# First layer's experts: both products of the 128-slot blocks from plain float32 operands

## What is computed

```python
logits = xf @ gate_w                        # 8 experts, each token takes its best 2
comb   = softmax weights of the best 2, scattered to (tokens, 8)
h   = gelu(einsum('nd,edf->enf', xf, W1) + b1[:, None, :], approximate=False)   # 256 -> 1024
y   = einsum('enf,efd->end', h, W2) + b2[:, None, :]                             # 1024 -> 256
out = einsum('ne,end->nd', comb, y)
```

## Time and profile before

| | |
|---|---|
| median of 3 runs | 838.35 us (836.78 to 839.5) |
| span of the profiled execution, first to last instruction | 836.6 us |
| first layer's experts, loads to last output issue | 225 to 497 us of the span |
| PE busy | 750.5 us (90%) |
| DVE busy | 609.3 us (73%) |
| ACT busy | 477.6 us (57%) |
| POOL busy | 386.1 us (46%) |

### The profile page before, as it was taken

How to read it: one execution, slowest core, us unless ns; L and a number is a source line. 1 busy time by engine, 2 the same in 40 slices (tenths; PEclk the granted TensorE clock), 3 DMA queues, 4 the chain that set the end, 5 groups by cost and what they waited for, 6 DMA issues and landing times. The chain is left out here.

```text
span 836.6 us, 17408 instructions
## 1 busy us (share of the span) xinstructions
PE 750.5 (90%) x6872; PEld 633.6 (76%) x6872; DVE 609.3 (73%) x1212; ACT 477.6 (57%) x722; POOL 386.1 (46%) x379
## 2 busy tenths in 40 slices
PE   6999999999469999999999948999999998359995
PEld 5666676667359999999999947667676667359995
DVE  4777776753769998998998925777776752869982
ACT  3386666654057776776776613586666753536640
POOL 5465444122145766666666335565542112183532
PEclk9999999999769999999999988999999999669998
DMA  7001000010286888888788327000000000477732
GB/s 227 16 27 40 27 17 13 28 52 27 71 308 199 260 253 259 257 255 258 250 244 261 89 33 228 14 15 27 15 15 14 15 15 26 154 263 244 214 86 28
DMA packets 45521, 101.35 MB, mean 121 GB/s; under 512 B 9824, under 2 KB 36064, under 8 KB 37760
## 3 DMA queue, kind: packets, MB, share of 16 engines
q0 software_dynamic: 16800, 65.46, 26.7%
q1 hardware_dynamic: 28640, 34.78, 12.7%
HBM read 84.22 MB, written 15.74 MB: 119 GB/s over the span
## 5 line engine op out<-in xcount | busy, mean ns | idle before, releaser
L600 DVE TENSOR_REDUCE mx_a<-ps_max_a 128x2 f32<-128x512 f32 x256 | 164.1, 684 | 35.4 <-PE ps_max_a L846 35.1
L89 PE MATMUL ps_h_e<-xe_t_e,w_e 128*128 128x256 f32 (+1 forms) x480 | 137.8, 287 | 9.8 <-DVE xe_t_e L1770 9.8
L452 ACT ACTIVATE prob_a<-ps_st_a 128x2048 f32<-128x2048 f32 x64 | 120.1, 1877 | 29.0 <-PE ps_st_a L865 28.6
L90 PE MATMUL ps_h_e<-xe_t_e,w_e 128*128 128x256 f32 (+1 forms) x480 | 134.6, 281 | 0.0
L91 PE MATMUL ps_h_e<-xe_t_e,w_e 128*128 128x256 f32 (+1 forms) x480 | 134.6, 280 | 0.0
L89 PE MATMUL ps_y_e<-w_e,h_e 128*128 128x256 f32 x424 | 118.2, 279 | 0.0
L91 PE MATMUL ps_y_e<-w_e,h_e 128*128 128x256 f32 x424 | 117.7, 278 | 0.0
L90 PE MATMUL ps_y_e<-w_e,h_e 128*128 128x256 f32 x424 | 117.7, 278 | 0.0
L89 PEld LDWEIGHTS ps_h_e<-xe_t_e,w_e 128*128 128x128 f32 x480 | 92.7, 193 | 12.3 <-DVE xe_t_e L1770 12.2
L91 PEld LDWEIGHTS ps_h_e<-xe_t_e,w_e 128*128 128x128 f32 x480 | 92.4, 193 | 0.0
L90 PEld LDWEIGHTS ps_h_e<-xe_t_e,w_e 128*128 128x128 f32 x480 | 92.3, 192 | 0.0
(11 more groups left out here) (234 smaller groups left out, 1763.1 us busy)
## 6 DMA issues: line engine op xcount, KB each, us to landing
w_raw_w<-L_w SPq DMA_DIRECT2D x14, 1024.0 KB, 6.6
ctx_raw_a<-ctx_t SPq DMA_DIRECT2D x16, 256.0 KB, 4.7
normalised_weighted<-xr SPq DMA_DIRECT2D x16, 256.0 KB, 2.2
x_sb<-x SPq DMA_DIRECT2D x8, 256.0 KB, 4.8
x_sb<-x SPq DMA_DIRECT2D x2, 1024.0 KB, 8.5
x<-x_sb SPq DMA_DIRECT2D x8, 256.0 KB, 2.5
out<-x_sb SPq DMA_DIRECT2D x4, 512.0 KB, 7.7
q_s_a<-m_t_a SPq DMA_DIRECT2D x64, 4.0 KB
```

Source lines behind the costliest of these rows:

```text
L89: pe.matmul(out, lhs[0], rhs[0], start=start, stop=False)
L90: pe.matmul(out, lhs[1], rhs[0], start=False, stop=False)
L452: act.activation(prob[n % 2][:, :, :, :], ps_st[:, :, :, :], ACT.Exp, scale=HD ** -0.5).then_inc(prob_ready, 1)
L600: dve.tensor_reduce(mx[:, q, h:h + HG + 1:HG], ps_max[j][:, :, :], AX.X, ALU.max).then_inc(max_done, 1)
```

## The change

In the first layer the seven small blocks take both products straight from unsplit float32 operands. The first product reads `w1_raw` and a plain copy of the transposed tokens (`xe_plain`), one matmul where `split_matmul` made three; the second reads a plain `h_plain`, which the gelu writes directly, and `w2_raw`. Nothing is rounded or subtracted for a small block: `w1_high`, `w1_low`, `w2_high`, `w2_low`, `hidden_parts` and the subtraction of `inputs_low` return at once; only the two bias copies stay on DVE. Since PE now reads the raw buffers, they are free later: `w1_raw` of a small block when its first product is done, `w2_raw` when its second is. POOL's order follows: `load_w1` of F2, which wants S's buffer, goes to the end of S's turn, and `load_w2` of F2 to the end of F1's turn. The full blocks and the second layer compute as before.

```diff
     xe_t = [[sb(f"xe_t{i}{j}", [P, KC, SB], F32R) for j in range(2)] for i in range(2)]
+    if layer == 0:
+        xe_plain = sb("xe_plain", [P, KC, P])
+    more = sb("more", [P, MORE])
+    h_plain = more[:, 0:FC * P].rearrange("p (j s) -> p j s", j=FC)
...
@@ -1569,11 +1580,15 @@
         def load_w1(b):
             if b < blocks:
                 pool.wait_ge(w1_ready, b - 1)
+                if small(b - 2):
+                    pool.wait_ge(h_ps, (b - 1) * NP)
                 gather_weights(pool, "w1", buffers, shared, dram, b)
 
         def load_w2(b):
             if b < blocks:
                 wait(pool, w2_ready, b - 1)
+                if b >= 2 and small(b - 2):
+                    pool.wait_ge(y_ps, b - 1)
                 gather_weights(pool, "w2", buffers, shared, dram, b)
...
         else:
             for b in range(blocks):
-                load_w1(b + 2)
-                load_w2(b + 1)
+                if not small(b):
+                    load_w1(b + 2)
+                if b == 0 or not small(b - 1):
+                    load_w2(b + 1)
                 load_x(b + 2)
                 if b >= 2:
                     add_to_tokens(b - 2)
+                if small(b):
+                    load_w1(b + 2)
+                if b and small(b - 1):
+                    load_w2(b + 1)
...
         def hidden(b, jp):
             act.wait_ge(h_ps, b * NP + jp + 1)
-            wait(act, h_ready, b * NP + jp - 1)
+            if small(b):
+                if jp == 0:
+                    wait(act, y_ps, max([c + 1 for c in range(b) if small(c)], default=0))
+                for j in range(2):
+                    ins = act.activation(h_plain[:, 2 * jp + j, :], ps_h[jp % RB][:, j, 0:P], ACT.Gelu,
+                                         bias=b1[b % 2][:, 2 * jp + j:2 * jp + j + 1])
+                ins.then_inc(hid_ready, 1)
+                return
...
         def inputs_high(b):
             act.wait_ge(xe_ps, b + 1)
-            w = order[b][2] * P
-            act.activation(xe_t[b % 2][0][:, :, 0:w], ps_x[b % 2][:, :, 0:w], ACT.Copy).then_inc(xe_hi, 1)
+            if small(b):
+                wait(act, h_ps, max([(c + 1) * NP for c in range(b) if small(c)], default=0))
+                act.activation(xe_plain[:, :, :], ps_x[b % 2][:, :, 0:P], ACT.Copy).then_inc(xe_hi, 1)
+            else:
+                act.activation(xe_t[b % 2][0][:, :, :], ps_x[b % 2][:, :, :], ACT.Copy).then_inc(xe_hi, 1)
...
     def dve_part(dve):
+        def small_bias(b):
+
+            dve.wait_ge(w1_ld[b % 2], loaded(b))
+            wait(dve, hid_ready, (b - 1) * NP)
+            dve.tensor_copy(b1[b % 2][:, :], w1_raw[b % 2][:, KC * F:KC * F + FC]).then_inc(w1_ready, 1)
+
         def w1_low(b, k):
-            dve.wait_ge(w1_hi, b * KC + k + 1)
+            if small(b):
+                if k == KC - 1:
+                    small_bias(b)
+                return
+            dve.wait_ge(w1_hi, splits(b) * KC + k + 1)
...
         def w2_low(b, k):
-            dve.wait_ge(w2_hi, b * 2 + k + 1)
+            if small(b):
+                if k == 1:
+                    dve.wait_ge(w2_ld[b % 2], loaded(b))
+                    wait(dve, y_biased, b - 1)
+                    dve.tensor_copy(b2[b % 2][:, :], w2_raw[b % 2][:, FC * D:FC * D + D]).then_inc(w2_ready, 1)
+                return
+            dve.wait_ge(w2_hi, splits(b) * 2 + k + 1)
...
         def hidden_parts(b, jp):
+            if small(b):
+                return
...
-                dve.tensor_reduce(slot_weight[:, b, 0:n], by_expert[:, 0:n, :], AX.X, ALU.add)
-            dve.tensor_tensor(xe_t[b % 2][1][:, :, 0:n * P], ps_x[b % 2][:, :, 0:n * P], xe_t[b % 2][0][:, :, 0:n * P].bitcast(F32),
-                              ALU.subtract).then_inc(xe_ready, 1)
+                ins = dve.tensor_reduce(slot_weight[:, b, 0:n], by_expert[:, 0:n, :], AX.X, ALU.add)
+            if not small(b):
+                ins = dve.tensor_tensor(xe_t[b % 2][1][:, :, :], ps_x[b % 2][:, :, :], xe_t[b % 2][0][:, :, :].bitcast(F32),
+                                        ALU.subtract)
+            ins.then_inc(xe_ready, 1)
...
                     for k in range(KC):
+                        if small(b):
+                            ins = pe.matmul(ps_h[jp % RB][:, j, 0:w],
+                                            w1_raw[b % 2][:, k * F + (2 * jp + j) * P:k * F + (2 * jp + j + 1) * P],
+                                            xe_plain[:, k, :], start=k == 0, stop=k == KC - 1)
+                            continue
                         ins = split_matmul(pe, ps_h[jp % RB][:, j, 0:w], [w1[b % 2][s][:, k, 2 * jp + j, :] for s in range(2)],
                                            [xe_t[b % 2][s][:, k, 0:w] for s in range(2)], k == 0, k == KC - 1)
...
         def second_product(b):
             pe.wait_ge(w2_ready, b + 1)
-            pe.wait_ge(h_ready, (b + 1) * NP)
+            if small(b):
+                pe.wait_ge(hid_ready, (b + 1) * NP)
+            else:
+                pe.wait_ge(h_ready, (splits(b) + 1) * NP)
             wait(pe, y_ready if layer else y_biased, b - 1)
...
                 for j in range(FC):
+                    if small(b):
+                        ins = pe.matmul(bank[:, q, :], h_plain[:, j, :], w2_raw[b % 2][:, j * D:(j + 1) * D], start=j == 0, stop=j == FC - 1)
+                        continue
                     ins = split_matmul(pe, bank[:, q, :], [h[b % 2][s][:, j, q * P:(q + 1) * P] for s in range(2)],
                                        [w2[b % 2][s][:, j, :] for s in range(2)], j == 0, j == FC - 1)
```

## The result

The changed kernel takes 853.09 us (median of 4 runs, 852.22 to 854.14), the kernel before beside it 837.98 us (4 runs): a ratio of 1.0176, 95% interval 1.016 to 1.0192, **15.1 us slower**. The forecast was slower by 4.3 us, 842.7, and a range that ended at 849. The direction was right and the size was not. In the profiled executions the span grew from 836.6 to 852.0 us, by 15.4.

What follows compares the result with a forecast made beforehand. It took the chain of loads and splits ending in F2's first product to set the small blocks' turns: +5.9 us for six late loads, -1.6 for the last block, +4.3 in sum, 842.7 us from 838.35; range 835 to 849.

Steps and rivals of the forecast that it cites:

- PE's records: Small block's products on PE: plain records 0.115 and 0.23 us each; first product saves 1.6 us, second loses 1.0.
- The removed work on ACT and DVE: Small blocks' copies and subtractions go, none on PE's path; DVE's busy time falls by more than 7 x 4.85 us.
- The late load: w1 of F2, issued last in S's turn of POOL, makes each of six turns 0.98 us longer: +5.9 us.
- w2 of F2 has room: w2 of F2, issued at 19.6 us, lands at 25.6; ACT wants it only in the third step of F2's turn.
- The tail: Last block, 22: first product 1.6 us shorter, longer second product hidden; -1.6 us.
- the clock: Rival: PE's clock falls at the waits, 0.9 us for each of six, +5.4 us more, 848.1 us; chance 0.04.
- the longer chain: Rival: back-to-back w1 loads make the chain to F2 1 us longer each turn, +6 us, 848.7 us; chance 0.08.
- The rival in which PE sets the pace: w1 of F2 in place by about 10.4 us, each turn 1.1 us shorter, 830.2 us; chance 0.17.

Runs made afterwards that it cites:

- E5: Changed kernel, but small blocks' weights land in memory of their own and all loads keep the order of the kernel before: 828.33 us beside 839.03.
- E3: Kernel before, all products still split, with only the loads moved and made to wait as in the change: 856.16 us beside 838.74.
- E8: E5 with w1 of F2 issued last in S's turn of POOL, as in the changed kernel: 852.82 us beside 838.53.
- E9: E5 with w2 of F2 issued last in F1's turn of POOL, as in the changed kernel: 827.90 us beside 838.53.
- E10: The changed kernel run again as it is: 852.71 us, beside 838.80 for the kernel before.
- E1: Changed kernel with 8 thrown-away plain matmuls on PE ahead of F2's wait: 850.38 us beside 838.74.
- E2: Changed kernel with the load of F2's w1 issued ahead of the two outputs in S's turn of POOL: 841.52 us beside 838.74.

## Why the prediction had the direction and not the size

- **PE's records: right, slightly too dear.** 24 records in 2.84 us are (2.84 - 0.28) / 23 = 0.111 us each with 128 columns, 16 in 3.62 are (3.62 - 0.38) / 15 = 0.216 with 256; 0.115 and 0.23 were taken. The first product saves 1.8 us (1.6 forecast), and PE alone brings F2 19.0 us after S, by E5, not 19.6. A plain matmul has two records, each with a load, and the first product's 32 take 1.8 us less than the 48 of halves. The Trainium skill ("FP8 and Floating Point Precision", section "TensorE Precision Notes") speaks of four passes for true float32; read as four loads it would have made this product 7.0 us, and the row excludes that: its 32 records at 0.111 us are 3.6 us.
- **The removed work on ACT and DVE: right.** DVE's busy time fell by 50.2 us (over 34 forecast), with nothing to show for it.
- **The late load: right in mechanism, place and nearly in size.** Issue after S 6.46 us forecast, 6.28 to 7.71 measured; transfer 6.0 forecast, 5.5 to 6.9 measured; `weigh` to F2 8.24 forecast, 8.21 measured. +5.9 forecast, +7.9 measured. The excess is in turns 3 and 10: at place 3 the issue came at 7.71; at place 10 POOL began 0.2 us later than forecast, its five issues took 0.3 us longer and the transfer 6.9 us in place of 6.0. E3, E5 and E8 show the load, and E8 and E9 show which. That ACT would wait 1 to 3 us for it was too little by far (44.5 us in six times): ACT's own work for S is short, so it stands there early.
- **w2 of F2 has room: right** (E9, nothing). **The tail: right**, -1.6 forecast and -1.8 found: the last output is issued 17.3 us after block 22's first matmul, where it was 19.05.
- **The step that failed is the clock.** The prediction had the row for it, an idle time of 1.92 us with a clock of 0.50 behind it, and its own waits were longer. It set it aside with "though between dense work", gave it 0.04 and put 0 into the sum. Dense work on both sides protected nothing: the clock fell behind four of six waits and cost 8.4 us in the profiled execution. Waits as short as the forecast ones, 2.1 us, were enough in other runs: it fell behind one of 2.08 us in E10 and two of 1.87 us in E8. Even the price in the rival was low, 5.4 us against 8.4. It took one loss of 0.9 us for each wait, "since the chain does not hang on PE there"; but from F2 to the next S PE is the bound, the low stretch lasts 3.4 or 6.8 us, and each one costs 1.6 or 2.6 us there.
- **The range** ended at 849 because the longer chain and the clock were weighed as alternatives. They have one cause, the wait, and behind longer waits the falls were more frequent (counts in the last section). For the profiled execution the missing terms add up: 840.9 forecast, +2.0 for the chain, +8.4 for the clock, +0.9 ahead of block 3 and -0.2 for the tail are 852.0 us. For the median the clock's share stays open, and it isn't all of the miss: E1, in which the clock stays at 1.00 up to block 22, is at 850.38 and so above the range too, though 4.6 us by which its profiled execution is longer than the changed kernel's behind block 22 would account for that.
- The rival in which PE sets the pace (830.2) was the right picture of a kernel that wasn't this one: with the load issued as early as before it is E5, 828.33.

## What to carry to other kernels

Before an operand is taken straight from a load buffer, ask what the copy did besides rounding: here it let go of the buffer a whole turn early, and that was worth more than its work. If the new form is cheaper for the engines, look for other memory for it, so that no load moves; the place of a load in a shared issuing queue, not its bytes, decided 24.5 us. And where a change opens waits like these, of about 2 us and more, on a TensorE that otherwise never stops, add the slower clock behind them to the sum of the same case and not to a rival.

## What the runs showed of the hardware

- The granted clock fell to 0.50 for 3.4 or 6.8 us behind waits of 2.49 to 3.69 us that had dense matmuls on both sides. The wait's length doesn't tell it alone: one of 2.36 us (place 7) had no fall, and in E10 the same kernel had its falls behind other turns (7 and 19, not 10). Counted over PE's waits ahead of F2 in all runs: behind all ten of 3.02 to 4.47 us, behind nine of fourteen of 1.87 to 2.66 us, behind none of 1.69 us or less. Matmuls whose result is thrown away kept it at 1.00.
- A weight gather of 1 MB, w1 of F2, took 5.5 to 6.9 us to land in the changed kernel, the one that POOL issued right behind it 8.0 to 8.6 us, and w1 of F2 8.4 and 8.7 us in two turns of E2.
- A DVE operation of 256 columns that takes 0.41 us took 2.8 us in six executions while POOL worked without a pause beside it.
